# An adapter with layer norm, then a conditional linear layer: the prologue rearranged around the second sample

## The reference, cut to what matters

```python
# x (32, 512, 512); W1 (10, 512, 128), W2 (10, 128, 512); W (32, 512, 512)
h = relu(x @ W1[a] + b1[a])
y = x + h @ W2[a] + b2[a]
normed = (y - mean(y)) * rsqrt(var(y) + 1e-5)      # over the 512 features
x1 = x + normed * gamma[a] + beta[a]
out = x1 + x1 @ W[g] + b[g]
```

## Time and profile before

| | |
|---|---|
| median of 3 runs | 620.67 us (618.24 to 621.05) |
| profiled execution | 621.52 us |
| its span, first to last instruction | 619.6 us |
| TensorE (PE) busy | 610.4 us, 99% |
| GpSimd (POOL) busy | 548.1 us, 88% |
| VectorE (DVE) busy | 522.8 us, 84% |
| ScalarE (ACT) busy | 510.6 us, 82% |
| DMA, mean over the span | 268 GB/s |
| chain that ended last, by engine | PE 35%, POOL 29%, ACT 14%, issue 10%, DVE 6%, DMA 3% |

### The profile page before, as it was taken

The page is one execution under the profiler, slowest core; times in us unless marked ns, Lnnn a source line. Parts: engine busy times, 40 slices in busy tenths (PEclk is TensorE's granted clock), DMA queues, the critical chain, the costliest instruction groups (busy, mean ns, idle before and its releaser), DMA issues.

```text
span 619.6 us, 10902 instructions
## 1 busy us (share of the span) xinstructions
PE 610.4 (99%) x2876; PEld 491.0 (79%) x2876; DVE 522.8 (84%) x1153; ACT 510.6 (82%) x769; POOL 548.1 (88%) x442
## 2 busy tenths in 40 slices
PE   9999999999999999999999999999999999999997
PEld 7667888887878787888787877877878887888786
DVE  1799898888998889898889888889898889898673
ACT  3768888889889889889889888888888889889770
POOL 3689999999999998999999999999999999999930
PEclk9999999999999999999999999999999999999999
DMA  8968998898998888988888997988988898897422
GB/s 299 236 205 277 312 302 286 250 294 261 308 299 272 269 281 268 312 276 295 263 295 261 305 300 246 286 286 270 307 295 274 274 297 253 302 303 264 163 85 103
DMA packets 125616, 166.25 MB, mean 268 GB/s; under 512 B 10866, under 2 KB 72316, under 8 KB 121488
## 3 DMA queue, kind: packets, MB, share of 16 engines
q1 hardware_dynamic: 94612, 150.12, 73.7%
q10 hardware_dynamic: 30972, 15.78, 9.0%
HBM read 132.17 MB, written 33.55 MB: 267 GB/s over the span
## 4 chain that ended last, share of the span: by engine, by line
PE 35%; POOL 29%; ACT 14%; issue 10%; DVE 6%; DMA 3%; SPq 2%; ACTq 1%; POOLq 0%; DVEq 0%
POOL xs_lo L375 8%; ACT norm L473 8%; POOL w_lo L402 7%; PE o_bank L807 7%; PE o_bank L805 6%; PE o_bank L806 6%; POOL x_tok L396 5%; POOL w_raw L386 3%; PE n_bank L823 3%; POOL w_lo L362 3%; DMA b_bc<-in_L_cond_b 2%; PE d_bank L836 2%; PE d_bank L805 2%; PE d_bank L807 2%; PE d_bank L806 2%
## 5 line engine op out<-in xcount | busy, mean ns | idle before, releaser
L805 PE MATMUL o_bank<-w_hi,x1T_hi 128*128 128x512 f32 x512 | 205.7, 402 | 0.9 <-DVE x1T_lo L706 0.8
L807 PE MATMUL o_bank<-w_hi,x1T_lo 128*128 128x512 f32 x512 | 200.5, 392 | 0.0
L806 PE MATMUL o_bank<-w_lo,x1T_hi 128*128 128x512 f32 x512 | 199.6, 390 | 0.0
L396 POOL TENSOR_TENSOR x_tok<-x_tok,b_bc 128x512 f32<-128x512 f32 x128 | 163.8, 1304 | 12.5 <-PE o_bank L885 7.6
L402 POOL TENSOR_TENSOR w_lo<-w_raw,w_hi 128x512 fp32r<-128x512 f32 x128 | 163.3, 1300 | 9.9 <-ACT w_hi L483 9.9
L473 ACT ACTIVATE norm<-y,neg_mean_rstd,rstd 128x512 f32<-128x512 f32 x127 | 151.2, 1267 | 1.1 <-DVE neg_mean_rstd L691 1.1
L641 DVE STREAM_TRANSPOSE xT<-x_quad 128x512 f32<-128x512 f32 x120 | 126.8, 1102 | 29.8 <-DMA x_quad<-in_x 29.8
L807 PEld LDWEIGHTS o_bank<-w_hi,x1T_lo 128*128 128x128 f32 x512 | 96.1, 188 | 21.0
L805 PEld LDWEIGHTS o_bank<-w_hi,x1T_hi 128*128 128x128 f32 x512 | 96.3, 188 | 20.5 <-issue 2.2
L490 ACT ACTIVATE x1T_hi<-n_bank,params 128x512 fp32r<-128x512 f32 x126 | 84.3, 688 | 33.9 <-DVE n_bank L700 19.6
L806 PEld LDWEIGHTS o_bank<-w_lo,x1T_hi 128*128 128x128 f32 x512 | 96.4, 188 | 17.9
(11 more groups left out here) (77 smaller groups left out, 800.0 us busy)
## 6 DMA issues: line engine op xcount, KB each, us to landing
w_raw<-in_L_cond_W SPq DMA_DIRECT2D x32, 1024.0 KB, 6.6
out<-out_half SPq DMA_DIRECT2D x63, 512.0 KB, 4.0
x_tok<-in_x SPq DMA_DIRECT2D x31, 1024.0 KB, 11.2
w_raw<-in_L_cond_W SPq DMA_DIRECT2D x64, 256.0 KB, 4.2
b_bc<-in_L_cond_b SPq DMA_DIRECT2D x64, 256.0 KB, 8.8
x_quad<-in_x SPq DMA_DIRECT2D x62, 256.0 KB, 3.7
x_quad<-in_x ACTq DMA_DIRECT2D x58, 256.0 KB, 10.6
x_tok<-in_x ACTq DMA_DIRECT2D x2, 256.0 KB, 3.2
```

The lines of the kernel that those rows point to most:

```text
L396: pool.tensor_tensor(x_tok[p][:, t, :], x_tok[p][:, t, :], b2_bc[p][:, :], ALU.add).then_inc(x_b2_done, 1)
L805: pe.matmul(acc, lhs_hi, rhs_hi, start=first, stop=False)
L806: pe.matmul(acc, lhs_hi, rhs_lo, start=False, stop=False)
L807: return pe.matmul(acc, lhs_lo, rhs_hi, start=False, stop=last)
```

## The change

Eight edits, all in the prologue and in the first whole step.

- SyncE: the four strips of sample 2 are issued ahead of the wait for the table; the b1 column of sample 1 is loaded by itself, as that of sample 0 is, and no longer waits for the table.
- The three row loads for the table go from ScalarE's queue to the head of GpSimd's, ahead of the identity's memset.
- TensorE: the table's transposes stand ahead of up 0; all four chunks of sample 1 are turned between up 0 and down 0; `keep_clock(8)` becomes 6, the three `keep_clock(2)` go, `keep_clock(12)` becomes 8.
- Up 1 writes `n_bank[1]` and not `d_bank[0]`, and doesn't wait for `y_done`.
- ScalarE copies all four chunks of sample 1; norm 0 of sample 0 goes ahead of relu 1, and norm 3 is ScalarE's too.
- VectorE: no copies and no norm 3; the first two stream transposes of sample 2 go from the end of step 1 to the place ahead of low part h 1; y 1 waits tile by tile for the norms.
- W2's low part of sample 0 has a semaphore of its own; the table's copy stands ahead of it on VectorE.
- Step 2: linear tiles 0 and 1 are computed together, chunk by chunk.

```diff
+        def up_bank(k):
+            return n_bank[1] if k.since(1) and not k.since(2) else d_bank[0]
...
@@ sync, prologue
             load_w(sample_id(1, 0, G), 0)
+            sp.dma_start(params[1][:, 2 * NC:NP], b1[bass.ds(lang1, 1)].rearrange("o a -> a o")
+                         ).then_inc(first_b1_in[1], 16)
+            load_x_quads(2, 0, range(NQ))
             sp.wait_ge(table_done, 1)
-            sp.dma_start(params[0][:, 0:2 * NC],
-                         param_table[:, bass.ds(lang0, 1), 0:2 * NC].rearrange("p o n -> p (o n)")
-                         ).then_inc(params_in[0], 16)
-            load_params(lang1, 1)
-
-            load_x_quads(2, 0, range(NQ))
+            for lang, p in ((lang0, 0), (lang1, 1)):
+                sp.dma_start(params[p][:, 0:2 * NC],
+                             param_table[:, bass.ds(lang, 1), 0:2 * NC].rearrange("p o n -> p (o n)")
+                             ).then_inc(params_in[p], 16)
@@ gpsimd
+            pool.dma_start(param_rows[:, 0, :], gamma).then_inc(rows_in, 16)
+            pool.dma_start(param_rows[:, 1, :], beta).then_inc(rows_in, 16)
+            pool.dma_start(param_rows[:, 2, 0:A], b1).then_inc(rows_in, 16)
             pool.memset(ident[:, :], 0.0).then_inc(ident_done, 1)
@@ scalar, relu
-                if k.since(1):
+                if k.since(2):
                     act.wait_ge(params_in[k.b], 16 * k.pairs(0) + 16)
                 else:
-                    act.wait_ge(first_b1_in, 16)
+                    act.wait_ge(first_b1_in[k.b], 16)
@@ scalar, prologue
-            act.dma_start(param_rows[:, 0, :], gamma).then_inc(rows_in, 16)
-            act.dma_start(param_rows[:, 1, :], beta).then_inc(rows_in, 16)
-            act.dma_start(param_rows[:, 2, 0:A], b1).then_inc(rows_in, 16)
...
             relu(k0)
-            copy_first_xT(1, 0)
-            copy_first_xT(1, 1)
-            high_w2_of_next(k0)
+            for c in range(NC):
+                copy_first_xT(1, c)
+            high_w2(1, 0)
             for t in range(NT):
                 square(k0, t)
             deviation(k0)
+            normalise(k1, 0)
             relu(k1)
-            for t in range(NT - 1):
+            for t in range(1, NT):
                 normalise(k1, t)
@@ vector
                 if k.since(1) and not k.since(2):
-                    dve.wait_ge(norm_done, NT)
+                    dve.wait_ge(norm_done, t + 1)
...
+            copy_table()
             dve.wait_ge(w2_hi_done, 1)
             dve.tensor_tensor(w2_lo[0][:, :], w2_raw[0][:, :], w2_hi[0][:, :].bitcast(F32), ALU.subtract
-                              ).then_inc(w2_lo_done, 1)
-            copy_table()
+                              ).then_inc(first_w2_lo_done, 1)
             low_h(k0)
             for t in range(NT):
                 y_tile(k0, t)
                 mean(k0, t)
-            dve.wait_ge(xT_done, NC + 2)
-            for c in (2, 3):
-                dve.wait_ge(first_xT_turned, NC + c + 1)
-                dve.tensor_copy(xT[1][:, c, :], first_xT_bank(c)[:, :]).then_inc(xT_done, 1)
             variance(k0)
             inverse_deviation(k0)
-            dve.wait_ge(rstd_done, 1)
-            for t in (3,):
-                dve.tensor_scalar(norm[:, t, :], y[:, t, :], rstd[:, t:t + 1], neg_mean_rstd[:, t:t + 1],
-                                  ALU.mult, ALU.add).then_inc(norm_done, 1)
+            turn_next_x(k1, 0)
+            turn_next_x(k1, 1)
             low_h(k1)
...
             inverse_deviation(k1)
-            turn_next_x(k1, 0)
-            turn_next_x(k1, 1)
             turn_next_x(k1, 2)
             turn_next_x(k1, 3)
@@ tensor
+            def first_linear_pair(k):
+                for t in range(2):
+                    pe.wait_ge(out_done, k.count(NT, 2, t - 1 + OUT_CREDIT))
+                for c in range(NC):
+                    pe.wait_ge(w_lo_done, k.count(NC, 2, c + 1))
+                    pe.wait_ge(x1_lo_done, k.count(NC, 2, c + 1))
+                    for t in range(2):
+                        tokens = slice(t * P, (t + 1) * P)
+                        ins = split_product(o_bank[t][:, :], x1T_hi[k.b][:, c, tokens], x1T_lo[k.b][:, c, tokens],
+                                            w_hi[k.b][:, c, :], w_lo[k.b][:, c, :], c == 0, c == NC - 1)
+                        if c == NC - 1:
+                            ins.then_inc(linear_done, 1)
...
-                    if t < NT - 1:
-                        keep_clock(2, y_bank[1])
...
-            keep_clock(8, y_bank[1])
+            keep_clock(6, y_bank[1])
             pe.wait_ge(ident_done, 3)
             turn_first_x()
-            up(k0)
             pe.wait_ge(rows_in, 48)
...
             ins.then_inc(table_turned, 1)
-            turn_second_x(0)
-            turn_second_x(1)
+            up(k0)
+            for c in range(NC):
+                turn_second_x(c)
             pe.wait_ge(table_done, 1)
             down(k0)
-            turn_second_x(2)
-            turn_second_x(3)
+            pe.wait_ge(xT_done, 2 * NC)
             up(k1)
             keep_clock(4, o_bank[1])
             down(k1)
             for c in range(NC):
                 turn_norm(k1, c)
-            keep_clock(12, o_bank[1])
+            keep_clock(8, o_bank[1])
```

More of the change, by code:

```diff
@@ L167, in adapter_then_conditional_linear @@
         first_x_in = [sem(f"first_x_in{t}") for t in range(NT - 1)]
-        first_b1_in = sem("first_b1_in")
+        first_b1_in = [sem(f"first_b1_in{i}") for i in range(2)]
         xq_in = [sem(f"xq_in{i}") for i in range(2)]
@@ L209, in adapter_then_conditional_linear @@
         w2_lo_done = sem("w2_lo_done")
+        first_w2_lo_done = sem("first_w2_lo_done")
         diag_done = sem("diag_done")
@@ L316, in _ @@
             sp.dma_start(params[0][:, 2 * NC:NP], b1[bass.ds(lang0, 1)].rearrange("o a -> a o")
-                         ).then_inc(first_b1_in, 16)
+                         ).then_inc(first_b1_in[0], 16)
             load_x(1, 1)
@@ L495, in relu @@
                 act.wait_ge(up_done, k.count(1, 0, 1))
-                if k.since(1):
+                if k.since(2):
                     act.wait_ge(params_in[k.b], 16 * k.pairs(0) + 16)
                 else:
-                    act.wait_ge(first_b1_in, 16)
-                act.activation(d_bank[0][:, :], d_bank[0][:, :], ACT.Relu,
+                    act.wait_ge(first_b1_in[k.b], 16)
+                act.activation(up_bank(k)[:, :], up_bank(k)[:, :], ACT.Relu,
                                bias=params[k.b][:, 2 * NC:NP]).then_inc(relu_done, 1)
                 act.wait_ge(relu_done, k.count(1, 0, 1))
-                act.activation(hT_hi[:, :], d_bank[0][:, :], ACT.Copy).then_inc(h_hi_done, 1)
+                act.activation(hT_hi[:, :], up_bank(k)[:, :], ACT.Copy).then_inc(h_hi_done, 1)
             def square(k, t):
@@ L645, in low_h @@
                 dve.wait_ge(h_hi_done, k.count(1, 0, 1))
-                dve.tensor_tensor(hT_lo[:, :], d_bank[0][:, :], hT_hi[:, :].bitcast(F32),
+                dve.tensor_tensor(hT_lo[:, :], up_bank(k)[:, :], hT_hi[:, :].bitcast(F32),
                                   ALU.subtract).then_inc(h_lo_done, 1)
@@ L828, in up @@
             def up(k):
-                acc, parts = d_bank[0][:, :], NS if k.since(3) else 0
+                acc, parts = up_bank(k)[:, :], NS if k.since(3) else 0
                 pe.wait_ge(w1_in[k.b], 16 * k.pairs(0) + 16)
-                if k.since(1):
+                if k.since(2):
                     pe.wait_ge(y_done, k.count(NT, 0, 0))
@@ L847, in down @@
                 pe.wait_ge(h_lo_done, k.count(1, 0, 1))
-                pe.wait_ge(w2_lo_done, k.count(1, 0, 1))
+                if k.since(1):
+                    pe.wait_ge(w2_lo_done, k.count(1, 0, 0))
+                else:
+                    pe.wait_ge(first_w2_lo_done, 1)
                 for t in range(NT):
@@ L864, in linear_tile @@
                 ins.then_inc(linear_done, 1)
+            def first_linear_pair(k):
[10 more added lines that the diff above has]
+                            ins.then_inc(linear_done, 1)
             def step(h, p):
                 k = Step(h, p)
-                linear_tile(k, 0)
-                linear_tile(k, 1)
+                if k.last(2):
+                    first_linear_pair(k)
+                else:
+                    linear_tile(k, 0)
+                    linear_tile(k, 1)
                 up(k)
```

## The result

Six executions of the changed kernel have a median of 622.22 us (619.78 to 623.44), six of the kernel before on the same chip 618.86 (618.23 to 621.05); the ratio is 1.0043, interval 1.0025 to 1.0061. On another chip, with ten executions against 27, it was 1.0022 (0.9998 to 1.0045). Forecast were 618.1 and a ratio of 0.996, with a range up to 620.7: the sign and the range are both wrong. The forecast started from 620.67, the median of three executions; over six it is 618.86, so that a gain of 2.6 us would have given 616.3.

The account below looks back on a forecast made before the run. The prediction took GpSimd's chain, nearly as long as a TensorE step, to set when step 3 starts. Start 0.8, copies -0.1, step 1 1.2, GpSimd's idle time 0.8 and DMA -0.1 gave 2.6 us: median 618.1, range 615.9 to 620.7.

Parts of the forecast that it names:

- Part 1: Start to the first up: up begins at about 8.55 instead of 9.36, 0.8 us earlier.
- Rival (a): At the start: TensorE's clock rises some 3 us later, 1.5 us lost, time 619.5; chance 0.18.
- Part 2: Up to down of sample 0: down starts at 14.4, 0.8 us earlier; ScalarE's two extra copies lose 0.1.
- Part 3: Step 1: down of sample 1 at 23.87 instead of 25.17; the step adds 1.2 us to the gain.
- rival b: Step 1: x of sample 2 lands at 22.5 and delays low part of h; time 619.4; chance 0.10.
- Part 4: Step 2: GpSimd's chain, not TensorE, sets step 3; GpSimd's lost idle time adds 0.8 us.
- GpSimd's idle time of 0.8 us: Step 2: GpSimd no longer waits for ScalarE ahead of its chain, a gain of 0.8 us.
- the returned wait: Ahead of step 3: TensorE waits for ScalarE's norm, giving back 1 us of its gain.
- The sum: Whole prologue: 0.8 - 0.1 + 1.2 + 0.8 - 0.1 = 2.6 us gained, median 618.1.
- (d): Start: slow GpSimd issues delay the identity, TensorE idles and stays at 1.2 GHz; 621 to 625 us; chance 0.07.

Follow-up runs that it names:

- g3: Kernel before with 6 dummy passes at the start instead of 16 and none between the tiles of x; 618.98 us, ratio 1.0006.
- e1: Changed kernel with 16 dummy passes at the start instead of 12; 618.97 us, ratio 1.0006.
- g2: Kernel before without the eight dummy passes between up 1 and down 1; 620.59 us, ratio 1.0025.
- g4: Changed kernel with VectorE doing low part h 1 ahead of sample 2's strips, no dummies added; 618.14 us, ratio 0.9997.
- e3: Changed kernel with 16 dummy passes at the start and 24 between up 1 and down 1; 619.04 us, ratio 0.9999.
- f1: e3 with the b1 column and the four strips of sample 2 issued ahead of W; 618.91 us, ratio 0.9990.
- g1: e3 with VectorE doing low part h 1 first and one stream transpose of sample 2 moved to step 1's end; 617.85 us, ratio 0.9981.
- h1: g1 with linear tiles 0 and 1 of step 2 one after the other again; 618.41 us, ratio 0.9986.
- h2: g1 with 12 dummy passes at the start instead of 16; 618.34 us, ratio 0.9993.
- f2: Kernel before with only linear tiles 0 and 1 of step 2 computed together, chunk by chunk; 619.31 us, ratio 1.0004.
- f3: Changed kernel run again, unedited, for a second trace; 620.47 us, ratio 1.0022.
- e2: Changed kernel with 24 dummy passes instead of 8 between up 1 and down 1; 620.18 us, ratio 1.0011.

## Why the prediction was wrong, point by point

- **Part 1, start.** Identity and GpSimd's issues: right (1.9 us taken, 1.7 measured, hidden). The pace: wrong in the first trace. The forecast let TensorE rise to 2.4 GHz during the tiles of x, as before, and called a gap of 0.4 us short; the gap was 0.84, and up 0 cost 2.15 us more than the earlier trace rows. Rival (a) named this and put it at 1.5 us. Of seven traces with a short start one has the late rise. The length of the gap alone doesn't decide it: g3 had 1.76 us of gap there and its up 0 at full pace. What does, how often it comes, and what it costs the median, isn't settled.
- **Part 2.** Up start to down start at full pace: 14.56 - 8.71 = 5.85 in e1, 5.83 forecast. Right.
- **Part 3, the step that failed.** Two terms on the way to down 1. First, the sum had nothing for a fall of the level there. The forecast's own numbers (up 1 ends 21.1, eight passes, down 1 at 23.87) make a gap of 1.9 us where the kernel before had 1.22; it used the 1.22 only to argue about the start, in rival (a), and never looked at this gap. At 2.0 to 2.1 us the level fell in more than half of the executions of g2 and g4, and g2 gives the price, 1.55 us of the median; of the changed kernel's 16 executions 12 fell. Second, the forecast let the strips land at 20.8 to 21.3, without a working, and took 0.1 off. Behind W they took 8.4 to 10.2 us from issue to landing and not 3.4 to 5.2, and in four traces with a fast start VectorE got them at 22.1 to 22.9, 1.0 to 2.4 us late (rival b, given 0.10).
- **Part 4.** GpSimd's idle time of 0.8 us, its chain as what sets step 3, the returned wait: right in the changed kernel's traces and in e1 to e3, f1, g1 and g4 (a wait of 1.08 to 1.38 us with late strips or a late W, 0.55 to 0.57 in g1 and g4). In h1 and h2 the idle time is back, 0.78 and 1.09 us, with the strips of sample 3 2.0 and 1.2 us late; the forecast had seen that they might be late and put nothing into the sum. For the pair it counted nothing either; f2 agrees, and the traces of h1 and h2 speak for it.
- **The sum.** It put step 3 at 60.0. The first trace is 4.5 us later: 3.1 by the start, 1.6 by the fall, 0.2 made good. f3 is 3.2 later: 1.7 at the start of down 1, by the strips, 1.5 by the fall. In g1 all of the sum arrives: step 3 at 60.06, 2.6 us before 62.66. Of that the median shows 1.2 (interval 0.5 to 1.8). The earlier start is thus kept in part only; since the rest of the span scatters by 4 us between traces, it can't be said from them where the remainder goes.
- **Chances.** Each rival was weighed alone, and they were not independent: a faster start makes VectorE want the strips before they land, late strips make the gap longer, and behind the longer gap the level falls. The first trace is (a), the later ones are (b); the fall ahead of down 1, which comes on top in both, stood in no rival. The median of 622.22 lies in the 621 to 625 of (d), but not by (d)'s mechanism: the identity stood at 3.75 us, not at 5.7 or later.

## What to carry to other kernels

When a change shortens one engine's work, write down every gap of TensorE that the new order leaves, and compare it with the longest gap that the old trace survived; dummies are part of the schedule and have to be counted again after each move. A transfer sent earlier lands earlier only if the queue ahead of it is short: put the landing of what stands ahead of it into the sum. And where a part of the code is untouched, compare the traces up to its start only, and leave the total to repeated runs.

## What was not expected of the hardware

- A gap of 2.0 to 2.1 us brought TensorE from 2.4 to 1.2 GHz in 7 of 10 (g2) and 7 of 12 executions (g4), counted by the mean clock, after 20 us of work with no wait over 0.5 us in the trace; 1.22 us in the kernel before did so in none of 120. In between, the table has three of 12 at 1.77 (e2) and one of 12 at 1.41 (e3), but also one of 12 in f1, whose trace has a gap of 0.23: a gap is known from one execution of each kernel only. The Trainium skill (TensorE: Matmul & The Clock Gate, "What's actually happening") has activity release a default low level; the traces agree, with a wait of 2.01 us in the first trace and 2.11 in g2's, after which the windows' granted clock is 0.50.
- The granted clock printed for the first microseconds is 1.00 in every trace, while the paces of dummies and transposes say 1.2 GHz; in the changed kernel's first trace, where the low pace lasted to 13.9 us, the windows print 1.00 for all of it. (The 8 in the page's second slice, 15 to 31 us, is the fall of down 1; f3, without a late rise, has it too.) The mean over the span doesn't show a late rise either: it is 0.997 in this trace and 0.997 in those of f3 and g2, which have the fall alone. By the paces alone it can be seen.
- GpSimd's three DMA issues took 0.68, 0.52 and 0.52 us; the same three took 0.62, 0.30 and 0.35 on ScalarE's queue before. Their rows landed 4.2 to 4.3 us after issue, and nobody waited for them. The Trainium skill (DMA: Bandwidth & Descriptors, "Latency and other measured facts") gives about 1 us to the first byte of such a transfer; no run here shows the first byte by itself.
- Of the four issues of strips in a row behind W, the third took 2.4 to 3.1 us in all traces with this order and the others 0.4 to 0.9; SyncE stood for as long and issued the fourth strip near 14 us. What the issue waits for isn't shown.
